# A gated recurrence on one core: output turns behind their product, seeds at other steps, a VectorE step of 16 instructions, and an idle product ahead of each candidate group

## The reference, cut to what matters

```python
    x = x + _L0_cond_ref(x, ...)      # out = sum_e w[e] * mask[e] * (gelu(x @ ew1[e]) @ ew2[e]) + shared
    x = x + _L1_cond_ref(cond, x, ...)
    def step(h, xs):                  # 1024 steps, one after the other
        z = sigmoid(xzt + h @ U_z + vz)
        r = sigmoid(xrt + h @ U_r + vr)
        hh = tanh(xht + r * h @ U + vh)
        h_new = (1.0 - z) * h + z * hh
```

## Time and profile before

| what | value |
|---|---|
| median of three runs (lowest, highest) | 1899.76 us (1898.28, 1903.29) |
| the profiled execution: its own time | 1901.32 us |
| the profiled execution: span from first to last instruction | 1899.4 us |
| mean granted TensorE clock of that execution | 0.991 of full speed |
| busy share of the span: PE, PEld, DVE, ACT, POOL | 98%, 86%, 77%, 38%, 10% |

### The profile page before, as it was taken

The page is one execution under the profiler, slowest core; times in us unless marked ns, Lnnn a source line. Parts: engine busy times, 40 slices in busy tenths (PEclk is TensorE's granted clock), DMA queues, the critical chain, the costliest instruction groups (busy, mean ns, idle before and its releaser), DMA issues.

```text
span 1899.4 us, 97811 instructions
## 1 busy us (share of the span) xinstructions
PE 1853.4 (98%) x38961; PEld 1633.5 (86%) x38962; DVE 1453.8 (77%) x11494; ACT 712.9 (38%) x3785; POOL 198.8 (10%) x515
## 2 busy tenths in 40 slices
PE   8999999999999999999999999999999999999988
PEld 8888888888898888988888888888988888888765
DVE  5687877778787786877778787787877878777776
ACT  4333433434333333333333334343433334333322
POOL 0110101101020110101101011010101101011000
PEclk9999999999999998999999999999999999999998
DMA  9000000000000000000000000000000000000000
GB/s 318 3 4 5 5 4 5 5 4 5 5 4 5 4 4 5 4 5 5 4 5 5 4 5 5 4 5 5 4 4 5 4 5 4 4 4 4 5 4 4
DMA packets 16903, 23.38 MB, mean 12 GB/s; under 512 B 3584, under 2 KB 15159, under 8 KB 16444
## 3 DMA queue, kind: packets, MB, share of 16 engines
q1 hardware_dynamic: 15280, 17.05, 2.6%
q10 hardware_dynamic: 1164, 0.07, 0.0%
HBM read 15.01 MB, written 2.10 MB: 9 GB/s over the span
## 4 chain that ended last, share of the span: by engine, by line
PE 89%; DVE 5%; ACT 3%; issue 2%; DMA 0%; SPq 0%; DVEq 0%
PE y_ps L736 18%; PE up_ps L718 18%; PE r_ps L841 13%; PE c_ps L841 12%; PE c_ps L820 6%; PE r_ps L820 6%; PE z_ps L841 5%; PE z_ps L850 4%; ACT rc_tanh_ps L403 3%; DVE h_cur L644 2%; DVE p_cur L618 1%; PE z_tanh_ps L758 1%; PE c_ps L752 1%; PE z_ps L752 1%; PE r_ps L752 1%
## 5 line engine op out<-in xcount | busy, mean ns | idle before, releaser
L718 PE MATMUL up_ps<-feat,up_w 128*128 128x128 f32 x2528 | 519.2, 302 | 0.3 <-DMA up_w<-in_L_cond_ew 0.3
L736 PE MATMUL y_ps<-hidden,down_w 128*128 128x128 f32 x2528 | 513.6, 300 | 0.0
L817 PEld LDWEIGHTS <-u_high 128*128 128x128 f16 x4096 | 400.7, 98 | 8.8 <-issue 0.8
L403 ACT ACTIVATE rc_tanh_ps<-r_ps 128x4 f32<-128x4 f32 x1024 | 161.8, 158 | 592.2 <-PE r_ps L841 592.1
L718 PEld LDWEIGHTS up_ps<-feat,up_w 128*128 128x128 f32 x2528 | 363.5, 190 | 1.4 <-ACT hidden L392 0.6
L736 PEld LDWEIGHTS y_ps<-hidden,down_w 128*128 128x128 f32 x2528 | 361.4, 190 | 0.4
L841 PEld LDWEIGHTS r_ps<-h_cur,u_mid 128*128 128x128 f16 x4096 | 253.5, 96 | 115.7 <-issue 54.4
L841 PEld LDWEIGHTS c_ps<-p_cur,u_mid 128*128 128x128 f16 x4096 | 253.5, 96 | 111.7 <-issue 33.3
L841 PE MATMUL r_ps<-h_cur,u_mid 128*128 128x20 bf16 (+5 forms) x4096 | 338.3, 179 | 0.0
L841 PE MATMUL c_ps<-p_cur,u_mid 128*128 128x40 bf16 (+10 forms) x4096 | 338.0, 180 | 0.0
L644 DVE TENSOR_TENSOR_SCAN h_cur<-rc_tanh_ps,blend 128x8 f32<-128x8 f32 x1024 | 177.7, 174 | 171.4 <-ACT rc_tanh_ps L403 169.8
(11 more groups left out here) (151 smaller groups left out, 3765.2 us busy)
## 6 DMA issues: line engine op xcount, KB each, us to landing
up_w<-in_L_cond_ew SPq DMA_DIRECT2D x4, 1024.0 KB, 9.7
down_w<-in_L_cond_ew SPq DMA_DIRECT2D x4, 1024.0 KB, 10.3
x_rows<-in_x SPq DMA_DIRECT2D x8, 256.0 KB, 5.2
out<-out_rows SPq DMA_DIRECT2D x128, 16.0 KB, 1.8
up_w<-in_L_cond_sw SPq DMA_DIRECT2D x1, 1024.0 KB, 12.4
down_w<-in_L_cond_sw SPq DMA_DIRECT2D x1, 1024.0 KB, 13.2
cf<-in_L_cond_C_r SPq DMA_DIRECT2D x1, 256.0 KB, 9.7
cf<-in_L_cond_C_z SPq DMA_DIRECT2D x1, 256.0 KB, 9.9
```

Of the source, the lines that this page charges most:

```text
L403: act.activation((tanh_r, tanh_z, c_now)[g].rearrange("p (m b) -> p m b", b=B), before_tanh, ACT.Tanh, scale=0.5 / GAIN).then_inc(act_done, 1)
L718: last = mm(up_ps[n % 2][:, 0:COLS], up_w[:, e, k, j * P:(j + 1) * P], feat[:, k, c * COLS:(c + 1) * COLS], start=(k == 0), stop=(k == KC ...
L736: last = mm(y_ps[:, m * COLS:(m + 1) * COLS], down_w[:, e, j, m * P:(m + 1) * P], hidden[:, n % TILES_HELD, :], start=False, stop=(m == KC ...
L817: pe.ldweights(w[:, g, k, m * P:(m + 1) * P])
```

## The change

- **Turns.** In the four windows with a TURN, the product now stands ahead of it. How many products a window takes is as before.
- **Seeds.** The second seed of the candidate bank moves from t = 26 to t = 28; the first stays at t = 24.
- **VectorE's step.** A memset of one element of a new tile `spare` stands ahead of `p_cur` in every step that has no seed or residual there. `p_cur` now waits for four semaphores: the reset tanh, the end of the previous step's `h_two` (H_HIGH16), the end of its `half_h` (`blended`), and `z_summed`, which is long past. The wait on `blended` ahead of the first `blend` is gone. The memset of `z_ps` waits for `p_low` too. Eight memsets of `spare` stand ahead of the first step.
- **Idle product.** In window 0 of every step but one a chunk (t = 57), a product of the bf16 identity with 96 columns, into columns of `y_ps` that nothing reads, stands behind the window's product and ahead of the candidate group's first weights.

```diff
+IDLE_SHORT = 96
+LEAD_PADS = 8
-    for slot in TURNS:
-        SIDE[slot].append((TURN, 0, 0))
+    places = lambda t, w: 1 + w - ((t, w) in TURNS)
...
+    for slot in TURNS:
+        SIDE[slot].append((TURN, 0, 0))
-    SEEDS = {(24, 0): (C, 0), (26, 0): (C, 1), (24, 1): (R, 0), (26, 1): (R, 1), (28, 1): (Z, 0), (30, 1): (Z, 1)}
+    c_seeds = [t for t in range(22, CT, 2) if t - 1 not in GELU_STEP][:KC]
+    SEEDS = {**{(t, 0): (C, m) for m, t in enumerate(c_seeds)}, (24, 1): (R, 0), (26, 1): (R, 1), (28, 1): (Z, 0), (30, 1): (Z, 1)}
...
+            for i in range(LEAD_PADS):
+                dve.memset(spare[:, 1 + i:2 + i], 0.0)
             for s in range(T):
+                if extras(s) == 0:
+                    dve.memset(spare[:, 0:1], 0.0)
                 dve.wait_ge(act_done, s * GATES + R + 1)
-                dve.wait_ge(part_ready, parts + H_HIGH)
+                dve.wait_ge(part_ready, parts + H_HIGH16 if s else parts + H_HIGH)
+                dve.wait_ge(blended, (s + 1) * BLEND_STEP)
+                dve.wait_ge(z_summed if s else warm_made, max(s, 1))
                 dve.scalar_tensor_tensor(p_cur[:, :, 0:B], sq(tanh_r), 1.0, sq(h_now), ALU.add, ALU.mult
...
                 dve.wait_ge(z_summed, s + 1)
+                dve.wait_ge(part_ready, parts + PARTS_STEP + P_LOW)
                 dve.memset(here[:, :, t, :], 0.0).then_inc(part_ready, 1)
                 dve.wait_ge(act_done, s * GATES + Z + 1)
-                dve.wait_ge(blended, (s + 1) * BLEND_STEP)
...
+            def idle_beside_y(columns):
+                mm(y_ps[:, KC * COLS:KC * COLS + columns], ident16[:, :], keep_warm[:, 0:columns],
+                   start=False, stop=True, skip_group_check=True)
...
                 side(c, t, 0)
+                if t != RESIDUAL_STEP:
+                    idle_beside_y(IDLE_SHORT)
                 load(C, HIGH_PRODUCTS[0])
```

More of the change, by code:

```diff
@@ L99, in moe_gru_kernel @@
         for w in range(2):
-            while units and len(SIDE[t, w]) < 1 + w:
+            while units and len(SIDE[t, w]) < places(t, w):
                 SIDE[t, w].append(units.pop(0))
@@ L113, in moe_gru_kernel @@
         for w in range(2):
-            while projections[w] and len(SIDE[t, w]) < 1 + w:
+            while projections[w] and len(SIDE[t, w]) < places(t, w):
                 SIDE[t, w].append((PROJECT, *projections[w].pop(0)))
     assert not any(projections.values())
-    SEEDS = {(24, 0): (C, 0), (26, 0): (C, 1), (24, 1): (R, 0), (26, 1): (R, 1), (28, 1): (Z, 0), (30, 1): (Z, 1)}
+    for slot in TURNS:
+        SIDE[slot].append((TURN, 0, 0))
+    c_seeds = [t for t in range(22, CT, 2) if t - 1 not in GELU_STEP][:KC]
+    SEEDS = {**{(t, 0): (C, m) for m, t in enumerate(c_seeds)}, (24, 1): (R, 0), (26, 1): (R, 1), (28, 1): (Z, 0), (30, 1): (Z, 1)}
     ROW_B1, ROW_BG, ROW_COND = 0, BR * HT, BR * HT + GATES * KC
@@ L165, in moe_gru_kernel @@
         uall = sb("uall", [P, 1])
+        spare = sb("spare", [P, 1 + LEAD_PADS])
         w_scale = sb("w_scale", [P, 1])
@@ L609, in side, with extras @@
                     residual(c + 1, window)
+            def extras(s):
+                c, t = divmod(s, CT)
+                between = ((t, 0), (t - 1, 1))
+                some = sum(slot in SEEDS or slot[0] == RESIDUAL_STEP for slot in between)
+                assert some <= 1
+                return some if c < CH - 1 else 0
+            for i in range(LEAD_PADS):
+                dve.memset(spare[:, 1 + i:2 + i], 0.0)
             sq = lambda ap: ap.rearrange("p (m b) -> p m b", b=B)
```

## The result

The changed kernel takes 1943.37 us (median of four runs, 1942.54 to 1944.92) against 1899.02 us for the kernel before on the same chip: ratio 1.0236, 95% interval 1.0219 to 1.0254, so 2.4% slower. The forecast was 1922 us. The time lies in the stated range, at its upper end; the direction and the mechanism held, and the loss was twice what was forecast (44 us for 22).

The account below looks back on a forecast made before the run. A step is a relay with a clean 1.776 us; only the 22.6 us above clean steps could be removed. From 1901.3, - 9.4 - 5.7 - 1.2 - 3 + 32.3 + 7.7 = 1922 us, 1.2% slower; range 1890 to 1945.

Parts of the forecast that it names:

- Rival 1: At p_cur: opening a block is hidden, as in 13 earlier cases; faster, 1882 us; chance 0.13.
- Rival 3: At p_cur: opening overlaps part of the half_h wait, only long ones cost, 0.1 to 0.2; 1887 to 1901 us; chance 0.07.
- Rival 2: Window 0: the idle product comes on the path, 1008 x 0.04 on top, about 1962 us; chance 0.05.
- the 0.21 that was named as its sign: First candidate product more than 0.21 behind p_cur's start would prove rival 2 right.
- Old crossings: Late scans, each first of a new VectorE instruction block, and what follows from them go: -9.4 us.
- Turns, seed: Transposes behind the product no longer delay turn steps, -5.7 us; seed at t = 28 costs nothing, -1.2 us.
- Clock: Idle product's activity where the PE clock fell gives back 3 of 5.6 us.
- Crossings: Blocks opening at p_cur every eighth step: 54 x 0.38 late plus 74 x 0.16, +32.3 us.
- The same waits in the other steps: p_cur in 384 steps with long half_h and no crossing: +0.02 each, +7.7 us (none to 23).
- The other VectorE edits: Spare memset, z_ps memset's wait on p_low, later first blend, lead memsets: covered by idle time, 0.
- Idle product: Window 0: about 0.04 of product fits ahead of the candidate group, 0 cost at 0.03 us of cover.

Follow-up runs that it names:

- e2: Changed kernel with 11 lead memsets in place of 8, no wait changed, so blocks begin at the spare memset: 1909.51 us, ratio to before 1.0049.
- e3: Changed kernel with 0 lead memsets in place of 8, no wait changed, so most blocks begin at the scan: 1946.54 us, ratio 1.0249.
- e1: Changed kernel with the half_h wait back ahead of the first blend, p_cur waiting for the scan, 9 lead memsets: 1900.59 us, ratio to before 1.0003.
- e7: e1 with the stand-alone wait ahead of the z_ps memset asking for p_cur in place of p_low: 1880.74 us, ratio to before 0.9892.
- e5: Changed kernel with only the half_h wait stand-alone ahead of p_cur, z_ps memset wait as in e7, 9 lead memsets: 1904.92 us, ratio 1.0022.
- e6: Changed kernel with a third stand-alone wait ahead of p_cur, no p_low wait at the z_ps memset, 7 lead memsets: 1990.71 us, ratio 1.0471.
- e8: e7 without the idle product: 1884.20 us, ratio to before 0.9910.
- e4: Changed kernel with VectorE's step and waits of the kernel before (14 instructions); turns, seeds and idle product kept: 1891.44 us, ratio 0.9954.

## Why the prediction was right, and where its sizes were off

Right were the direction, the place and the mechanism: a block that begins behind a stand-alone wait starts to be opened only when that wait is passed. e2 and e3 show it by moving the boundary alone. The pattern came as forecast too: at t = 4, 12, 36 and 44 scan to scan is 2.18 (median; 2.15 forecast), at t = 20, 28, 52 and 60 it is 1.96 to 1.98 (1.94 forecast), and no scan is late. Rival 1 (hidden at `p_cur`) named its condition rightly: the opening must begin early. In the changed kernel it does not. In e1 and e7, where the last stand-alone wait ahead of `p_cur` is for the scan's end, it does, and all 128 crossings cost nothing. Rival 3 needed the opening to overlap the wait for `half_h`. It did not: at a crossing, whether `half_h` is long or short, `p_cur` starts 0.456 behind its end with one stand-alone wait (e5), 0.553 with two and 0.651 with three (e6, medians). The late scans of e3 start 0.455 behind the end of the second `blend`, with one such wait. Rival 2 fell. The first candidate product starts 0.215 behind `p_cur` with the idle product (e7) and without (e8), and 0.216 in the kernel before, so the 0.21 that was named as its sign was met already.

Term by term:

- *Old crossings* (-9.4): gone, the changed kernel has no late scan.
- *Turns, seed* (-5.7, -1.2): gone as forecast in the trace; with the clock, 9.1 us in e4 for 9.9.
- *Clock* (-3): the changed kernel has no slow stretch between 60 and 1930 us, so nearly all of the 5.6 us came back. e8 against e7 puts the idle product at 3.5 us. What took away the rest is not shown.
- *Crossings* (+32.3): measured 36.7. The counts were 58 and 70 for 54 and 74, the sizes 0.41 and 0.18 for 0.38 and 0.16.
- *The same waits in the other steps* (+7.7): measured 22.3. **This is the term that was mis-sized.** The second stand-alone wait was put at 0.06, the middle between 0.02 and 0.10, "as no row is nearer". e5 and e6 measure 0.10, the upper bound. The row for it was in the trace all along: the earlier trace rows is a stand-alone wait, and there was no reason why a second one should be cheaper than the first. The 0.04 of difference comes 401 times in the open (384 had been counted), and 0.03 and 0.02 of it stand at the crossings.
- *The other VectorE edits* (0): this held for the blends, with 0.05 us to spare (the second blend ends at 900.47 by the changed kernel's trace, a stand-alone wait takes 0.10, the scan starts at 900.63); e1 shows how near it was. It did not hold for the memset of `z_ps`. The prediction looked at what VectorE does behind the memset and not at who waits for it: TensorE's projections at t = 60 and 61, 2.8 us, for which the sum had nothing.
- *Idle product* (0): at t = 0, where the update group has more products, it lies on the path: the first candidate product starts 0.065 later than in other steps, in place of 0.023 in the kernel before and in e8. So its own cost is the estimated 0.04, 15 times.

With these sizes the forecast of 1922 becomes 1922 + 14.6 + 4.4 + 2.8 + 0.6 - 2.6 (the clock) = 1941.8 us, for 1942.75 us of the profiled execution; the scans start 1.0 us later in it than before (56.5 for 55.5). One error of 14.6 us thus makes most of the miss.

## What to carry to other kernels

Count the instructions of an engine that runs an unrolled loop, with the waits that stand alone, and look what stands at the block boundary and which stand-alone wait is the last ahead of it: here that decided 37 us in 1900, and a few empty instructions at the start of the program move it. A wait that is already satisfied is not free where it stands alone behind one that is not; place it where the engine has slack, or make the late wait the one that the instruction carries (a carried wait took 0.03 in the earlier trace rows; no run here moved one so). And when a wait is added, list who waits for that instruction on every engine, in the rare steps too.

## What was not expected of the hardware

Stand-alone waits add up in series, 0.10 us each behind the late one (0, 0.057 and 0.151 late with one, two and three), although those that follow had long been satisfied. The Trainium skill, in "Perfetto Trace Analysis", section "Identifying Dependency Chains", says that such instructions may be inserted ahead of one that waits for several engines. The traces agree: in the changed kernel two of them stand ahead of `p_cur`, on lines 635 and 636.

The long `half_h` follows GpSimd: the scaling takes 900.95 to 901.35, and `half_h`, begun at 900.99, ends at 901.38. All 459 long ones of the changed kernel lie beside a scaling that began 0.03 to 0.04 before them. Beside a scaling of 0.26 (t = 11 of chunk 4, from 548.30) `half_h` takes 0.24; at 58.62, where the scaling begins 0.05 behind it, it takes 0.17, and that scaling its usual 0.40. In "SBUF — State Buffer", section "SBUF: two separate sides", the Trainium skill says that GpSimd and some VectorE operations share a port pair, and that whichever starts first has it for its whole instruction. The rows on `half_h` fit this. The scaling behind 58.62 does not show it, as it is no longer than usual, and no row tells whether `half_h` is one of those operations.
